# When the engines' registers are loaded in two mixture-of-experts parts: one value per tile behind four first ones, in place of thirteen at a time

## The chip, the cores and the metric

The kernel runs on one core of one Trainium2 chip. Its time is the device time of one execution in microseconds (us). "Time before" is the median of three runs. The profile is of one further execution.

## The reference, cut to what matters

The program is one long chain of eight residual parts on 2048 tokens of 128 values: a state-space (Mamba) part, a top-2 mixture of eight experts, a linear attention, a gated top-2 mixture of eight experts, and four more parts. Only the two mixtures hold the change. For each token they choose two of eight experts, and add the weighted sum of those experts' answers:

```python
def body(acc, p):                      # first mixture: relu, with biases
    w1e, b1e, w2e, b2e, ce = p
    h = jax.nn.relu(xf @ w1e + b1e)    # 128 -> 512
    y = h @ w2e + b2e                  # 512 -> 128
    return (acc + y * ce[:, None], None)
...
def body(acc, inputs):                 # second mixture: gated, no biases
    wg, wu, wd, w = inputs
    h = jax.nn.silu(xf @ wg) * (xf @ wu)
    acc = acc + w[:, None] * (h @ wd)
    return (acc, None)
```

The weight `ce` or `w` of a token is zero for all but its two experts, so a kernel may compute only those two.

## The kernel before, in words

Each mixture has a routing and an expert part. The routing finds the two experts of every token and its place in a list sorted by expert. GpSimd (POOL) then sends each token's row to its two places in a DRAM tensor, `slots`, with 32 indirect DMAs (`scatter`). The list is cut into tiles of 128 rows, so that each tile belongs to one expert. There are at most NT = 2 * 16 + 8 - 1 = 39 tiles, and the program always runs 39.

Which expert a tile belongs to is known only at run time. VectorE (DVE) computes two tables of 39 integers each in SBUF: `whoi`, the expert of each tile, and `basei`, the tile's first row in `slots`. `s_table` counts 2 when both are there. An engine that wants to use such an integer in an address must first have it in one of its own registers. `values(...)` does this: it emits one register load (TENSOR_LOAD, all of them at line L1407) for a stretch of a table on one engine. Three engines need it: SyncE (SP) for the row in `slots` that its DMA reads, DVE for the expert whose weights it copies and whose biases it adds, and TensorE (PE) for the expert whose `wd` it reads. On PE the load stands in the stream of the engine's sequencer, which the trace calls PEldq.

The function `experts` runs the two expert parts, the first with `gated` false, the second with `gated` true. For tile i the steps are:

- SP: `dma_start(xg[i] <- slots)`, L1431, 12 buffers (NB). From tile 12 on it waits until the answer of tile i - 12 has gone out.
- PE `turn_x` (L1521): transposes the rows. ScalarE (ACT) takes them out of PSUM (L1470).
- DVE `copy_weights` (L1612 and L1613): copies the expert's weights to a fixed place, `wac` (and `wuc` in the gated part), 2 buffers. It goes by the register with the expert of tile i.
- PE `hidden` (L1528, and L1534 in the gated part): the first product. It waits for the transposed rows and for `wac` (`s_wc`).
- DVE `inner` (L1626 or L1621) with ACT relu (L1480) or silu (L1475): the activation.
- PE `down` (L1543): the second product, whose weights are addressed by the register with the tile's expert.
- DVE `weigh` (L1639 or L1634), in the first part ACT `share_of` (L1487) too; POOL sends the answers out (L1457).

The engines run a software pipeline, written out in program order per engine. In step i PE does `turn_x(i + 2)`, `hidden(i + 1)`, `down(i - 1)`, and DVE does `copy_weights(i + 2)`, `inner(i + 1)`, `weigh(i - 1)`. Each engine's sequencer takes its instructions in order: what stands behind a register load is not given to the engine before the load is done. What was given before it goes on.

Before the change each engine loads its 39 values in three groups of 13. DVE loads right ahead of `copy_weights` of tiles 0, 13 and 26, PE ahead of `down` of tiles 13 and 26 (and once at the start), SP ahead of the DMA of tiles 0, 13 and 26. In the second part DVE also has memsets for the next part behind `weigh`, from `early.zeros` (`next(zeros, None)`).

Of the kernel before, what the change touches and what calls it, by code (L numbers as in the profile page):

```python
# [30 lines left out]
ENGINE = mybir.EngineType  # L31
EVERY_ENGINE = [ENGINE.PE, ENGINE.Activation, ENGINE.Pool, ENGINE.DVE, ENGINE.SP]

P = 128
# [8 lines left out]
class Core:  # L43
# [76 lines left out]
    def sb(self, name, shape, dt=F32, ctx=None):  # L120
        return (ctx or self.ctx).enter_context(self.nc.sbuf_tensor(name, shape, dt))

    def sem(self, name):
        handle = self.nc.alloc_semaphore(name=name)
        self.part_sems.append(handle)
        return handle
# [1207 lines left out]
def experts(k, r, early, first):  # L1334


    nc, t, C, T, E = k.nc, k.t, k.C, k.T, k.E
# [2 lines left out]
    FB = F // P  # L1340
    ROW = k.ROW
    NT = 2 * T + E - 1
    NB, NY, NH, GROUP = 12, 6, 3, 13
    slots, answers = k.slots[name], k.answers[name]
    tmp = ExitStack()
    sb = lambda n, shape, dt=F32: k.sb(f"{name}_{n}", shape, dt, tmp)
# [2 lines left out]
    def wait(engine, sem, count):  # L1349

        if count > 0:
            engine.wait_ge(sem, count)

    with tmp:
# [12 lines left out]
        whoi, basei = sb("whoi", [P, NT], U32), sb("basei", [P, NT], U32)  # L1367
        xg = sb("xg", [P, NB, ROW])
# [19 lines left out]
        s_ld = [sem(f"load{b}") for b in range(NB)]  # L1388
# [8 lines left out]
        def loaded(engine, i):  # L1397
            engine.wait_ge(s_ld[i % NB], 16 * (i // NB + 1))

        def sent_out(engine, i):  # L1400
            if i >= 0:
                engine.wait_ge(s_out[i % NY], 16 * (i // NY + 1))

        def values(engine, table, i, top_value):

            reason = "counted up to the number of tiles, and the expert is held below their number"
            return nc.values_load_multi_w_load_instructions(  # L1407
                table[0:1, i:min(i + GROUP, NT)], engines=[engine], min_val=0, max_val=top_value,
                skip_runtime_bounds_check_because=reason)[1]

        def fetch_answers(engine, j):
            rows_of_all = answers[j * k.N:(j + 1) * k.N, :].rearrange("(p t) d -> p t d", t=T)
            for c in range(C):
                engine.dma_start(back[:, c, j], rows_of_all[:, of(c), :]).then_inc(s_back[c], 16)

        with nc.Block() as block:
            @block.sync
            def _(sp):
                for dst, src in weights:
                    sp.dma_start(dst, src).then_inc(s_w, 16)  # L1420
                if early:
                    early.load(sp)

                sp.wait_ge(s_table, 2)
                for i in range(NT):
                    if i % GROUP == 0:
                        rows_of = values(ENGINE.SP, basei, i, slots.shape[0] - P)
                    if i == 0:
                        sp.wait_ge(r.s_sent, 16 * 2 * T)
                    sent_out(sp, i - NB)  # L1430
                    sp.dma_start(xg[:, i % NB, :], slots[bass.ds(rows_of[i % GROUP], P), :]).then_inc(s_ld[i % NB], 16)  # L1431
                for i in range(NT - NY, NT):
                    sent_out(sp, i)
                fetch_answers(sp, 0)
                for c in range(C):
                    sp.wait_ge(s_back[c], 16 * 2)
# [69 lines left out]
            @block.tensor  # L1506
            def _(pe):
                for c in range(first, C):
                    r.ranks(pe, c)
                    if c + 1 < C:  # L1510
                        r.turn(pe, c + 1)
                        r.gate(pe, c + 1)
                pe.wait_ge(r.s_pick, C + 1)
                nc.tensor.matmul(bank[5][:, 0:E], k.onesb[:], r.before[:, C, :], start=True, stop=True).then_inc(r.s_rank, 1)

                experts_of = {}

                def turn_x(i):
                    loaded(pe, i)
                    wait(pe, s_xT, i)  # L1520
                    nc.tensor.transpose(bank[0][:, 0:P], xg[:, i % NB, 0:P], k.ident[:]).then_inc(s_tx, 1)  # L1521

                def hidden(i):
                    pe.wait_ge(s_xT, i + 1)
                    pe.wait_ge(s_wc, i + 1)
                    wait(pe, s_h1, i - 1)
                    for f in range(FB):
                        last = nc.tensor.matmul(bank[1 + i % 2][:, f * P:(f + 1) * P], wac[:, i % 2, f * P:(f + 1) * P],  # L1528
                                                xgT[:, i % 2, :], start=True, stop=True)
                    last.then_inc(s_g, 1)  # L1530
                    if gated:
                        wait(pe, s_hT, i - 1)
                        for f in range(FB):
                            last = nc.tensor.matmul(bank[3 + i % 2][:, f * P:(f + 1) * P], wuc[:, i % 2, f * P:(f + 1) * P],  # L1534
                                                    xgT[:, i % 2, :], start=True, stop=True)
                        last.then_inc(s_u, 1)

                def down(i):
                    pe.wait_ge(s_hT, i + 1)
                    wait(pe, y_read, i - 1)  # L1540
                    one = bass.ds(experts_of[i], 1)
                    for f in range(FB):
                        last = nc.tensor.matmul(bank[6 + i % 2][:, 0:P], hT[:, i % NH, f, :],  # L1543
                                                wd[:, one, f, :].rearrange("p o d -> p (o d)"),
                                                start=(f == 0), stop=(f == FB - 1))
                    last.then_inc(s_y, 1)

                pe.wait_ge(s_w, 16 * len(weights))
                pe.wait_ge(s_table, 2)
                experts_of.update(enumerate(values(ENGINE.PE, whoi, 0, E - 1)))  # L1550
                for i in range(-2, NT + 1):
                    if 0 <= i + 2 < NT:
                        turn_x(i + 2)
                    if 0 <= i + 1 < NT:
                        hidden(i + 1)
                    if 0 <= i - 1:
                        if i > 1 and (i - 1) % GROUP == 0:
                            experts_of.update(enumerate(values(ENGINE.PE, whoi, i - 1, E - 1), i - 1))
                        down(i - 1)

            @block.vector
            def _(dve):
# [42 lines left out]
                experts_of = {}  # L1605

                def copy_weights(i):
                    one = bass.ds(experts_of[i], 1)
                    flat = lambda w: w[:, one, :].rearrange("p o f -> p (o f)")
                    wait(dve, hidden_done, i - 1)  # L1610
                    if gated:
                        v.tensor_copy(wuc[:, i % 2, :], flat(wu))  # L1612
                    v.tensor_copy(wac[:, i % 2, :], flat(wa)).then_inc(s_wc, 1)  # L1613
# [15 lines left out]
                def weigh(i):  # L1629
                    dve.wait_ge(s_y, i + 1)  # L1630
                    if gated:
                        loaded(dve, i)
                        sent_out(dve, i - NY)
                        v.tensor_scalar(yw[:, i % NY, :], bank[6 + i % 2][:, 0:P], xg[:, i % NB, P + 1:P + 2], None, ALU.mult)\  # L1634
                            .then_inc(s_yw, 1)
                    else:
                        wait(dve, s_yw, i - 1)
                        bias = bd[:, bass.ds(experts_of[i], 1), :].rearrange("p o d -> p (o d)")
                        v.tensor_tensor(yb[:, i % 2, :], bank[6 + i % 2][:, 0:P], bias, ALU.add).then_inc(s_yb, 1)  # L1639

                dve.wait_ge(s_w, 16 * len(weights))
                dve.wait_ge(s_table, 2)
                zeros = early.zeros(v) if early else iter(())
                for i in range(-2, NT + 1):
                    if 0 <= i + 2 < NT:
                        if (i + 2) % GROUP == 0:
                            experts_of.update(enumerate(values(ENGINE.DVE, whoi, i + 2, E - 1), i + 2))
                        copy_weights(i + 2)
                    if 0 <= i + 1 < NT:
                        inner(i + 1)  # L1650
                    if 0 <= i - 1:
                        weigh(i - 1)
                    if i >= 0:
                        next(zeros, None)

# [1585 lines left out]
def program(nc, t, out):  # L3241
    with ExitStack() as ctx:
        k = Core(nc, ctx, t)
        routing = Routing(k, "moe0", gated=False)
        mamba(k, routing)
        k.part_sems += routing.sems
        experts(k, routing, None, first=1)
        k.end_part()

# [133 lines left out]
```

## Time and profile before

| | |
|---|---|
| time, median of 3 runs | 1362.14 us (1360.49 to 1362.29) |
| span of the profiled execution | 1358.3 us, 3.8 us under that median |
| the profiled execution's own time outside its span | not given; the span is all that the page has of it |
| PE busy | 79% of the span |
| DVE busy | 65% |
| ACT busy | 50% |
| POOL busy | 41% |
| first expert part, PE from the first to the last transposed tile | 372.4 to 453.7 us |
| gated expert part, the same | 570.8 to 681.9 us |

"Busy" counts the instructions of the engines. Register loads and other sequencer work are not counted, so such a load shows as idle time of the engine behind it, with "issue" as the releaser or with the last semaphore that was waited for before. The letter q behind an engine's name marks its sequencer. "PEld" is the weight load of TensorE, which runs ahead of its matmul.

### The profile page before, as it was taken

The numbers are of one execution on the slowest core, as the hardware profiler recorded it, in microseconds if no ns is written. First come the engines' busy times: TensorE is split into PE (matmuls) and PEld (weight loads), VectorE is DVE, ScalarE is ACT, GpSimd is POOL, SyncE is SP. The second block draws the span as 40 slices with busy tenths as digits, with TensorE's granted clock in tenths as the row PEclk, the third lists the DMA queues.
The fourth block names the chain that finished last, engine by engine and source line by source line (L and its number), as shares of the span: only waits on it lengthen the run. The fifth ranks groups of instructions, "written<-read, shape, count | busy, mean of one in ns | idle before, by whom it ended". The sixth has DMA issues, their size and how long they took to land. (4 is left out here: it accounts for less than half of the span.)

```text
span 1358.3 us, 25046 instructions
## 1 busy us (share of the span) xinstructions
PE 1079.5 (79%) x8292; PEld 708.4 (52%) x8292; DVE 881.0 (65%) x2989; ACT 685.8 (50%) x1268; POOL 559.6 (41%) x740
## 2 busy tenths in 40 slices
PE   8877777778189553299936999969977999899998
PEld 3222232336188553299934777744434777654544
DVE  6799999976455456377549888843648878840201
ACT  4786656644044301133206888737856888541221
POOL 4489988853633314544426444100025555100000
PEclk9799999998599765599978999989997999999999
DMA  2997000002422206211120000020612000000000
GB/s 63 206 202 126 0 1 0 1 0 71 140 61 57 92 7 219 70 41 44 37 74 1 2 3 3 2 53 6 203 47 89 3 2 3 2 1 0 16 0 16
DMA packets 85742, 66.77 MB, mean 49 GB/s; under 512 B 15102, under 2 KB 70412, under 8 KB 85612
## 3 DMA queue, kind: packets, MB, share of 16 engines
q1 hardware_dynamic: 79916, 53.65, 17.3%
q0 software_dynamic: 4544, 9.38, 1.9%
q10 hardware_dynamic: 1152, 2.10, 0.4%
q8 instruction: 70, 1.15, 0.4%
q14 instruction: 60, 0.49, 0.1%
HBM read 36.52 MB, written 28.59 MB: 48 GB/s over the span
## 5 line engine op out<-in xcount | busy, mean ns | idle before, releaser
L1076 POOL TENSOR_TENSOR hC<-h,Cs 128x1024 f32<-128x1024 f32 x64 | 150.8, 2356 | 35.3 <-DVE h L973 34.7
L786 PE MATMUL bank<-hC,ident 128*128 128x512 f32 x256 | 128.1, 624 | 45.1 <-POOL hC L1076 43.0
L973 DVE TENSOR_TENSOR_SCAN h<-bank,state,dBx 128x512 f32<-128x512 f32 x128 | 157.3, 1271 | 2.2
L1457 POOL DMA_INDIRECT moe_answers<-moe_yw,moe_xg x78 | 83.7, 1073 | 128.9 <-DVE moe_yw L1634 70.9
L2608 DVE CUSTOM_DVE_ANT_0 decay_below<-bank,decay_q_mask 128x256 bf16<-128x256 f32 x256 | 97.3, 419 | 23.3 <-PE bank L2420 22.4
L786 PEld LDWEIGHTS bank<-hC,ident 128*128 128x128 f32 x256 | 44.9, 192 | 103.9 <-POOL hC L1076 67.1
L2608 DVE CUSTOM_DVE_ANT_0 window_below<-bank,window_q_mask 128x192 bf16<-128x192 f32 x256 | 80.3, 353 | 28.6 <-PE bank L2420 27.0
L2548 ACT ACTIVATE decay_pb<-bank 128x512 f32<-128x512 f32 x128 | 76.2, 598 | 33.5 <-PE bank L2435 32.6
L885 ACT ACTIVATE bank<-dt,A 128x512 f32<-128x512 f32 x128 | 83.2, 683 | 18.7 <-DVE h L973 17.4
L1528 PE MATMUL bank<-moe_xgT,moe_wac 128*128 128x128 f32 x624 | 86.4, 284 | 6.5 <-issue 4.0
L1543 PE MATMUL bank<-moe_wd,moe_hT 128*128 x624 | 83.2, 278 | 5.7 <-DVE moe_hT L1621 2.5
L1528 PEld LDWEIGHTS bank<-moe_xgT,moe_wac 128*128 128x128 f32 x624 | 79.5, 200 | 7.4 <-issue 4.5
L1543 PEld LDWEIGHTS bank<-moe_wd,moe_hT 128*128 128x128 f32 x624 | 76.5, 193 | 6.5 <-issue 6.5
L2548 ACT ACTIVATE window_pb<-bank 128x384 f32<-128x384 f32 x128 | 62.3, 491 | 34.4 <-PE bank L2435 32.4
L3235 DVE TENSOR_TENSOR f_ys<-bank,f_s 128x256 f32<-128x256 f32 x8 | 3.4, 425 | 117.3 <-PE bank L3178 117.3
L1330 POOL DMA_INDIRECT moe_slots<-moe_rows,moe_slot x64 | 62.3, 973 | 31.1 <-issue 16.6
L241 POOL TENSOR_TENSOR rstd<-veps,mhalf 128x4 f32<-128x4 f32 (+1 forms) x12 | 14.8, 1237 | 138.9 <-DVE veps L235 138.9
L1470 ACT ACTIVATE moe_xgT<-bank 128x128 f32<-128x128 f32 x78 | 20.9, 268 | 97.7 <-PE bank L1521 97.5
L963 DVE TENSOR_TENSOR dBx<-dtx,bank 128x768 f32<-128x768 f32 (+1 forms) x64 | 65.2, 1019 | 1.2 <-PE bank L766 0.7
L910 ACT ACTIVATE Cs<-bank 128x512 f32<-128x512 f32 x64 | 38.1, 596 | 39.0 <-POOL hC L1076 31.4
L1521 PE MATMUL bank<-ident,moe_xg 128*128 128x128 f32 x78 | 22.5, 288 | 43.0 <-DMA moe_xg<-moe_slots 41.7
L3169 PE MATMUL bank<-f_hA,f_h1w 128*128 128x512 f32 x128 | 55.3, 592 | 0.0
(482 smaller groups left out, 2797.2 us busy)
## 6 DMA issues: line engine op xcount, KB each, us to landing
moe_slots<-blank SPq DMA_DIRECT2D x16, 1040.0 KB, 16.9
deep_rows<-token_weights SPq DMA_DIRECT2D x32, 256.0 KB, 3.9
moe_xg<-moe_slots SPq DMA_DIRECT2D x78, 65.0 KB, 1.9
moe_wa<-in_moe_w SPq DMA_DIRECT2D x2, 2048.0 KB, 9.7
moe_back<-moe_answers SPq DMA_DIRECT2D x8, 256.0 KB, 5.3
moe_back<-moe_answers ACTq DMA_DIRECT2D x8, 256.0 KB, 6.0
moe_wu<-in_moe_wu SPq DMA_DIRECT2D x1, 2048.0 KB, 15.4
deep_w<-in_deep_w SPq DMA_DIRECT2D x3, 512.0 KB, 6.5
```

The source lines that it names most:

```text
L786: last = nc.tensor.matmul(sum_bank(hh)[:], k.ident[:], hC[:, u % 2, hh, :], start=(n == 0), stop=(n == NS - 1))
L885: nc.scalar.activation(decay_bank(u, hh)[:], dt[:, hh, cols(c)], ACT.Exp, scale=A[:, hh, n:n + 1]).then_inc(q_dA, 1)
L963: v.tensor_tensor(dBx[:, u % 2, :, 0:w], dtx[:, :, c * CW:c * CW + w], b_bank[:, None, 0:w].to_broadcast([P, H, w]), ALU.mult).then_inc(q_ ...
L973: v.tensor_tensor_scan(h[:, u % 2, hh, :], decay_bank(u, hh)[:], dBx[:, u % 2, hh, :], state[:, n, hh:hh + 1], ALU.mult, ALU.add).then_inc ...
L1076: g.tensor_tensor(hC[:, u % 2], h[:, u % 2], Cs[:, u % 2, None, :].to_broadcast([P, H, CW]), ALU.mult).then_inc(q_hC, 1)
L1330: k.nc.gpsimd.indirect_dma_start(k.slots[self.name], index, self.rows[j][:, i, :], None)\
L1457: nc.gpsimd.indirect_dma_start(answers, bass.IndirectOffsetOnAxis(index, 0), yw[:, i % NY, :], None)\
L1528: last = nc.tensor.matmul(bank[1 + i % 2][:, f * P:(f + 1) * P], wac[:, i % 2, f * P:(f + 1) * P], xgT[:, i % 2, :], start=True, stop=True)
L1543: last = nc.tensor.matmul(bank[6 + i % 2][:, 0:P], hT[:, i % NH, f, :], wd[:, one, f, :].rearrange("p o d -> p (o d)"), start=(f == 0), st ...
L2548: nc.scalar.activation(pb[:, w % 4, :], bank[2 + w % 2][:, 0:2 * HW], ACT.Exp).then_inc(s_ex, 1)
L2608: last = nc.vector.tensor_tensor_reduce(out=below[:, 2 * g + j, :], in0=bank[g % 2][:, j * HW:(j + 1) * HW], in1=q_mask[:], scale=-1.0, sc ...
L3169: last = k.nc.tensor.matmul(bank[4 + m % 4][:], self.hw[layer][:, i, f * P:(f + 1) * P], src[:, i, :], start=(i == 0), stop=(i == FB - 1))
```

## The change

The number GROUP = 13 goes, and LEAD = 4 comes. Each of the three engines first loads the values of tiles 0 to 3 in one load. The values of tiles 4 to 38 are then loaded one at a time. SP loads the one of tile i ahead of that tile's DMA (and ahead of its wait for tile i - 12). PE and DVE load the one of tile i + 3 at the end of step i, behind `down(i - 1)` and `weigh(i - 1)`. For DVE this is right ahead of `copy_weights` of the same tile in step i + 1; for PE it is three steps and more ahead of `down` of that tile.

```diff
-    NB, NY, NH, GROUP = 12, 6, 3, 13
+    NB, NY, NH, LEAD = 12, 6, 3, 4
...
-        def values(engine, table, i, top_value):
+        def values(engine, table, i, m, top_value):
...
-                table[0:1, i:min(i + GROUP, NT)], engines=[engine], min_val=0, max_val=top_value,
+                table[0:1, i:i + m], engines=[engine], min_val=0, max_val=top_value,
...
+                rows_of = dict(enumerate(values(ENGINE.SP, basei, 0, LEAD, slots.shape[0] - P)))
                 for i in range(NT):
-                    if i % GROUP == 0:
-                        rows_of = values(ENGINE.SP, basei, i, slots.shape[0] - P)
+                    if i >= LEAD:
+                        rows_of[i] = values(ENGINE.SP, basei, i, 1, slots.shape[0] - P)[0]
...
-                experts_of.update(enumerate(values(ENGINE.PE, whoi, 0, E - 1)))
+                experts_of.update(enumerate(values(ENGINE.PE, whoi, 0, LEAD, E - 1)))
...
                     if 0 <= i - 1:
-                        if i > 1 and (i - 1) % GROUP == 0:
-                            experts_of.update(enumerate(values(ENGINE.PE, whoi, i - 1, E - 1), i - 1))
                         down(i - 1)
+                    if LEAD <= i + 3 < NT:
+                        experts_of[i + 3] = values(ENGINE.PE, whoi, i + 3, 1, E - 1)[0]
...
+                experts_of.update(enumerate(values(ENGINE.DVE, whoi, 0, LEAD, E - 1)))
...
                     if 0 <= i + 2 < NT:
-                        if (i + 2) % GROUP == 0:
-                            experts_of.update(enumerate(values(ENGINE.DVE, whoi, i + 2, E - 1), i + 2))
                         copy_weights(i + 2)
...
                     if 0 <= i - 1:
                         weigh(i - 1)
+                    if LEAD <= i + 3 < NT:
+                        experts_of[i + 3] = values(ENGINE.DVE, whoi, i + 3, 1, E - 1)[0]
                     if i >= 0:
                         next(zeros, None)
```

## Rows read from the trace of the kernel before

**Rows 1.** The head of the page.

```profile
span 1358.3 us, 25046 instructions
```

**Rows 2.** Waits of PE, 379 to 455 us: total us, times, longest.

```profile
PE bank L1528 <- issue: 4.0, 2, 2.1
PE bank L1543 <- ACT moe_hT L1480: 1.9, 1, 1.9
PE bank L1543 <- issue: 1.3, 1, 1.3
```

**Rows 3.** The same view, 578 to 683 us.

```profile
PE bank L1543 <- DVE moe_hT L1621: 2.5, 2, 1.3
PE bank L1528 <- ACT moe_xgT L1470: 2.5, 2, 1.3
```

**Rows 4.** L1521 on PE in four stretches: min/median/max ns, first to last start.

```profile
L1521 PE MATMUL bank<-ident,moe_xg x35: 272/273/421, 379.3 to 453.7; 128*128 128x128 f32 x35
...
L1521 PE MATMUL bank<-ident,moe_xg x10: 272/273/273, 408.4 to 425.5; 128*128 128x128 f32 x10
...
L1521 PE MATMUL bank<-ident,moe_xg x36: 272/273/273, 578.3 to 681.9; 128*128 128x128 f32 x36
...
L1521 PE MATMUL bank<-ident,moe_xg x9: 272/273/273, 620.4 to 642.7; 128*128 128x128 f32 x9
```

**Rows 5.** Register loads of L1407: three engines, whole span; two single ones.

```profile
L1407 SPq TENSOR_LOAD <-moe_basei x6: 1304/2757/2770, 358.9 to 624.4; - x6
L1407 DVEq TENSOR_LOAD <-moe_whoi x6: 1144/3010/3209, 359.0 to 645.7; - x6
L1407 PEldq TENSOR_LOAD <-moe_whoi x6: 1257/3127/3194, 359.0 to 655.2; - x6
...
L1407 DVEq TENSOR_LOAD <-moe_whoi x1: 3141/3141/3141, 396.7 to 396.7; - x1
...
L1407 PEldq TENSOR_LOAD <-moe_whoi x1: 3194/3194/3194, 403.9 to 403.9; - x1
```

**Rows 6.** Register loads of one value, L2814, a later part of the kernel.

```profile
L2814 SPq TENSOR_LOAD <-blank x1: 277/277/277, 908.8 to 908.8; - x1
...
L2814 DVEq TENSOR_LOAD <-blank x1: 308/308/308, 908.8 to 908.8; - x1
L2814 PEldq TENSOR_LOAD <-blank x1: 306/306/306, 908.9 to 908.9; - x1
```

**Rows 7.** Timeline at a load of DVE: start, duration, [idle before].

```profile
400.01 0.43 DVE L1613 COPY moe_wac<-moe_wa 128x512 f32 x1 [3.03 <-issue]
...
400.50 0.97 PEld L1528 LDWEIGHTS bank<-moe_xgT,moe_wac 128*128 128x128 f32 x8 [2.20 <-issue]
```

**Rows 8.** Busy time in a stretch; behind POOL, the granted clock.

```profile
430.50:434.00 3.50, 3.50 (x19) 3.50 (x19) 1.62 (x4) 2.00 (x6) 1.92 (x2) 0.53 0.16 45
```

**Rows 9.** Timeline of an undisturbed tile, first part: DVE, then PEld.

```profile
412.50 0.29 DVE L1639 TENSOR_TENSOR moe_yb<-bank,moe_bd 128x128 f32<-128x128 f32 x1 [0.20 <-PE bank L1543]
412.70 0.42 DVE L1613 COPY moe_wac<-moe_wa 128x512 f32 x1
...
414.08 0.41 PEld L1528 LDWEIGHTS bank<-moe_xgT,moe_wac 128*128 128x128 f32 x3
```

**Rows 10.** Timeline of an undisturbed tile, gated part: DVE, then PEld.

```profile
614.62 0.41 DVE L1613 COPY moe_wac<-moe_wa 128x512 f32 x1
...
616.12 0.30 PEld L1528 LDWEIGHTS bank<-moe_xgT,moe_wac 128*128 128x128 f32 x2
```

**Rows 11.** PE's sequencer, same tile as rows 9: `down`'s last address work, next waits.

```profile
L1543 PEldq FUSED_REGOPS  x1: 46/46/46, 412.4 to 412.4; - x1
...
L1352 PEldq EVENT_SEMAPHORE  x2: 51/51/51, 413.4 to 413.6; - x2
```

**Rows 12.** SP's DMA issues of L1431: first twelve tiles, the other 27.

```profile
L1431 SPq DMA_DIRECT2D moe_xg<-moe_slots x12: 333/333/353, 370.5 to 376.7; - x12
...
L1431 SPq DMA_DIRECT2D moe_xg<-moe_slots x27: 332/333/333, 384.9 to 444.1; - x27
```

More of the change, by code:

```diff
@@ L1430, in _ @@
                     sent_out(sp, i - NB)
-                    sp.dma_start(xg[:, i % NB, :], slots[bass.ds(rows_of[i % GROUP], P), :]).then_inc(s_ld[i % NB], 16)
+                    sp.dma_start(xg[:, i % NB, :], slots[bass.ds(rows_of[i], P), :]).then_inc(s_ld[i % NB], 16)
                 for i in range(NT - NY, NT):
```

## The prediction

> **What bounds the kernel now.** The page gives a span of 1358.3 us [rows 1]; the median of the runs shown is 1362.14 us, 3.8 us more. The change touches only the two expert parts, so I read those. The first view is the waits of PE, once for each part. In the first part, from the fifth tile on, PE is idle four times for 4.0 + 1.9 + 1.3 = 7.2 us [rows 2]; in the gated part four times for 5.0 us [rows 3]. There are no other waits of PE in either stretch. So outside these eight places PE sets the pace, and whatever is taken from it comes off the end: nothing of the next part starts before the last tile is through.
>
> The second view says what a stall costs, its after-effects included: the starts of PE's transposes, of which each tile has one. Undisturbed, nine intervals take 425.5 - 408.4 = 17.1 us, 1.90 us a tile; in the gated part eight take 22.3 us, 2.79 us a tile [rows 4]. The first part has 34 intervals from 379.3 to 453.7 us, 74.4 us; at 1.90 they would take 64.6 us, so 9.8 us are lost. The gated part has 35 from 578.3 to 681.9 us, 103.6 us; at 2.79 they would take 97.6 us, so 6.0 us are lost. The sum is 15.8 us.
>
> The third view says who causes it: the register loads. In each part every engine has three, so four of each engine's six stand in mid-loop; the median shows that these take about 3.0 us on DVE and 3.1 us on PE, whereas those before the loops take from 1.1 us on [rows 5]. One of DVE's runs from 396.7 for 3.14 us, to 399.85; the copy of the weights behind it starts at 400.01, and PE's weight load that needs the copy at 400.50 [rows 5, 7]. The page puts "issue" there because no semaphore was late, only the sequencer. One of PE's runs from 403.9 to 407.1 us, and `down` stands behind it [rows 5]; that is the 1.9 us put down to ACT [rows 2], whose value had long been there. Two engines with two such loads in each of two parts make eight, which is the count of PE's waits.
>
> PE's idle time is 12.2 us and the loss 15.8 us. A part of the difference is the clock: from 430.5 to 434.0 us, just after the second stall by DVE (PE had been idle for about 2 us), the granted clock was 0.53 [rows 8], near the lower level of 1.2 GHz, with PE busy all the time. That disappears with its stall.
>
> **Removed.** Two mid-loop loads of 13 values on each engine and part. On PE and DVE they cost the 15.8 us above. On SP they take 2.76 us, but SP's last transfer is issued at 444.1 us for a tile that PE turns at 453.7 [rows 4, 12], a lead of 9.6 us: nothing is won there. The gain is 15.8 us if what is added is covered.
>
> **Added.** 35 loads of one value on each of three engines in each part. The price of one: the only ones of one value in the trace took 0.277 (SP), 0.308 (DVE) and 0.306 us (PE), with idle engines [rows 6]. Thirteen in mid-loop took 2.76 us on SP, so twelve more values cost 2.48 us, 0.21 us each. On a working DVE thirteen took 3.14 us, 1.14 times SP's price. I take 0.308 x 1.14 = 0.35 us for DVE and PE. The bounds are 0.28 us below, and above 1.14 us, the shortest load in the expert parts [rows 5], of 13 values. The single loads are far nearer in kind, hence 0.35. In the sum of its loads DVE gets more sequencer time, about 35 x 0.35 = 12 us a part for some 7.5 (two of 3.1 and the first one) [rows 5]; what counts is where it lies.
>
> *DVE, first part.* The load stands behind `weigh`, which is given out at 412.50, and pushes back the copy behind it, which ends at 413.12 [rows 9]. PE's weight load wants that copy at 414.08. In the stall the copy ended at 400.44 and the weight load began at 400.50 [rows 7], so it needs 0.06 to 0.07 us. Cover: 414.08 - 0.07 - 413.12 = 0.89 us. With 0.35 us the copy ends at 413.47, while PE's sequencer comes to its own waits at 413.4 to 413.6 anyway [rows 11]. The load costs nothing and 0.54 us of cover is left. Behind the load in the queue are the copy, the next bias addition and the next `weigh`. A load longer than 0.89 us costs PE its excess at every tile.
>
> *DVE, gated part.* The same reckoning: copy done at 615.03, wanted at 616.12 less 0.07 [rows 10]. Cover 1.02 us, nothing lost. The memsets behind the load write tiles of a later part.
>
> *PE.* The sequencer has done the last address work of `down` at 412.4 us and next does something at 413.4, the waits for the turned rows and the copy [rows 11]. The load falls into this stretch of about 0.9 us, in which it waits anyway. Beyond that, the engine has work in its queue until the weight load at 414.08 that starts the next `hidden` [rows 9]. Cover about 1.5 us. The value is needed by `down` three steps later. Cost nothing.
>
> *SP.* Twelve transfers went out in 6.2 us [rows 12]. Eight of them now have a load ahead: 8 x 0.28 = 2.2 us more, so the twelfth leaves at 378.9 in place of 376.7 us, for the twelfth tile, which is turned at 379.3 + 7 x 1.90 = 392.6 us [rows 4]. From tile 12 on, the load stands ahead of the wait for a free buffer, and falls into that wait. Cost nothing.
>
> *The first load*, of four in place of 13 values, ends sooner. SP issues its first transfer only at 370.5 us, when the table has been read for ten microseconds [rows 5, 12], since the rows must have been scattered. Gain nothing.
>
> The Trainium skill speaks against the change: "DMA: Bandwidth & Descriptors", section Latency and other measured facts, puts a floor of some 600 ns under a tensor_load and says that loads are grouped to amortize it. The rows of one value lie at half of that [rows 6]. By the page, as an estimate, the added loads would take 0.6 us, DVE's cover in the first part would shrink to 0.29 us, and the time would be the same as long as nothing else lies in it.
>
> **The sum.** 1358.3 - 15.8 + 0 = 1342.5 us of span, and 1362.1 - 15.8 = 1346.3 us of time.
>
> **The rivals.**
>
> *The loads on a busy engine are dearer, and part of the gain leaks.* For: on DVE and PE thirteen values took 0.25 to 0.45 us longer than on SP, and the rows of one value are from idle engines; if that surplus is a fixed price per load, one takes 0.6 to 0.75 us. Against: even that is under 0.89. At the upper bound, 1.14 us, each tile of the first part loses 0.25 us and each gated one 0.12: 35 x 0.37 = 13.0 us, and the time is 1359.3 us. Chance 0.12 for 1351.5 to 1359.3 us, and 0.05 for the little beyond that ends within 0.2% of the time before.
>
> *The other side: a load in mid-loop has its price per load, not per value.* Then a single one on DVE takes 3.14 us in the first part and 3.01 in the gated one, and holds back the copies of every tile: 35 x (3.14 - 0.89) + 35 x (3.01 - 1.02) = 78.8 + 69.7 = 148.5 us, less 15.8, so 1495 us. It decides from 35 x (d - 0.89) + 35 x (d - 1.02) = 15.8 on, which is d = 1.18 us; from 1.22 us on the kernel is slower by over 0.2%. For: 13 values took 1.1 to 1.4 us in one place and 3.0 to 3.2 in another, so something beside their number matters. Against: SP, which has nothing else to do, shows the same factor of two with hardly any scatter, so that it is not the load on the engine, and one value took 0.3. Chance 0.05.
>
> *The clock's fall is not the stall's.* Then 3.5 x (1 - 0.53) = 1.6 us remain [rows 8], and it is 1347.9 us. Against: it followed upon an idle PE. It lies within the range of the likeliest case.
>
> **How the numbers follow.** The likeliest case, full cover, has 0.78: 1346.3 us, from 1344 (the three runs before differ by 1.8 us) to 1351.5 us (about 0.07 us lost at each of 70 tiles). The leaks have 0.17, the dear load 0.05. The range of eight in ten is the likeliest one's. Within 0.2%, 2.7 us, a measurement of this kernel can't tell a change from none. Faster 0.78 + 0.12 = 0.90, same 0.05, slower 0.05.
>
> **What would show it.** Right: transposes 1.90 and 2.79 us apart throughout; no wait of PE over some tenths in either stretch; loads of one value of 0.3 to 0.4 us, the first part's copy of the weights later by that, its end still ahead of PE; no stretch at half clock after 378 us. The step on the price is wrong if DVE's single loads take over 0.9 us; the step on the cover is wrong if the copy waits longer than the load or the tile interval grows by even 0.1 us. The prediction fails if SP's lead at the end is gone, or if the transposes still have gaps at tiles 13 and 26.

## The result, and the profile after

The changed kernel takes 1347.95 us (median of four runs, 1346.86 to 1349.12), the kernel before took 1361.9 us beside it (1360.49 to 1362.29). The ratio is 0.9898, with a 95% interval of 0.9881 to 0.9916: faster by 1.0%, or 13.95 us. The forecast was 1346.3 us, in a range of 1344.0 to 1351.5. In the changed kernel the lines behind the loop of SP are one higher: L1521 is L1522, L1613 is L1614, and so on.

The head of the page, and PE's waits from the fifth tile on in the first part (380 to 446 us) and in the gated part (567 to 667 us). The second view has its header and no row; it was the same for both stretches.

```profile
span 1345.2 us, 25235 instructions
```

```profile
core 0 of [0], span 1345.2 us
engine line waited for: us in total, times, longest us
```

Before, these stretches had eight waits and 12.2 us [rows 2, 3]. None is left. The transposes, again with the first and the last start of each stretch:

```profile
L1522 PE MATMUL bank<-ident,moe_xg x35: 272/273/273, 379.6 to 444.1; 128*128 128x128 f32 x35
...
L1522 PE MATMUL bank<-ident,moe_xg x36: 272/273/273, 567.4 to 665.0; 128*128 128x128 f32 x36
```

The 34 intervals take 64.5 us where they took 74.4, and the 35 gated ones 97.6 where they took 103.6 [rows 4]. So 9.9 + 6.0 = 15.9 us came from just where the sum put 15.8. The register loads of L1407:

```profile
L1407 SPq TENSOR_LOAD <-moe_basei x72: 268/277/497, 358.2 to 644.6; - x72
L1407 DVEq TENSOR_LOAD <-moe_whoi x72: 300/304/646, 358.2 to 665.2; - x72
L1407 PEldq TENSOR_LOAD <-moe_whoi x72: 295/302/567, 358.3 to 663.0; - x72
```

There are twelve times as many as before [rows 5]; the medians are 0.28 us on SP and 0.30 us on DVE and PE, as the idle engines' loads of one value took [rows 6]. The timeline of one tile of the first part shows how the load on DVE is covered (DVE's rows, then PEld's):

```profile
402.67 0.29 DVE L1640 TENSOR_TENSOR moe_yb<-bank,moe_bd 128x128 f32<-128x128 f32 x1 [0.20 <-PE bank L1544]
403.17 0.43 DVE L1614 COPY moe_wac<-moe_wa 128x512 f32 x1 [0.20 <-issue]
...
404.26 0.41 PEld L1529 LDWEIGHTS bank<-moe_xgT,moe_wac 128*128 128x128 f32 x3
```

The copy starts 0.50 us after the start of `weigh`, in place of 0.20 [rows 9]: later by the 0.30 us of the load. Only 0.20 us of it show as idle time ("issue"); the rest runs beside `weigh`. The copy ends at 403.60, and PE takes it up at 404.26, so 0.59 us of cover is left after the 0.07 us of hand-over, where the forecast said 0.54. SP's issues:

```profile
L1432 SPq DMA_DIRECT2D moe_xg<-moe_slots x12: 333/333/353, 369.9 to 378.5; - x12
...
L1432 SPq DMA_DIRECT2D moe_xg<-moe_slots x39: 332/333/353, 369.9 to 434.8; - x39
```

Twelve take 8.6 us in place of 6.2 [rows 12], 2.4 us more for 2.2 forecast, and the last leaves 9.3 us ahead of the last transpose: SP's loads cost nothing either.

**Where 2.8 us of the span are.** The span fell by 1358.3 - 1345.2 = 13.1 us, not by 15.9. From the last transpose of the gated part to the end it was 1358.3 - 681.9 = 676.4 us before and 1345.2 - 665.0 = 680.2 us after, 3.8 us more, in parts that the change does not touch; the stretches outside these three are together 1.0 us shorter. One piece of them is longer too, at the start of the first part: the interval behind the fourth transpose (376.7 to 379.6 us) took 2.9 us, where it was 2.0 us before (377.3 to 379.3 us). In the windows of the two intervals, the changed kernel's first, the last three columns are granted clock, DMA share and GB/s:

```profile
376.70:379.60 2.90, 2.90 (x18) 2.82 (x18) 1.59 (x3) 0.80 (x2) 0.00 (x0) 0.67 0.36 79
```

```profile
377.33:379.32 1.99, 1.99 (x18) 1.99 (x19) 1.28 (x3) 0.79 (x2) 0.00 (x0) 1.00 0.28 68
```

In the changed kernel the clock was still at its lower level of 1.2 GHz for most of it, after the engine had idled for 21 us ahead of the part; before, it was at its higher level throughout. Whether this and the 3.8 us belong to the change was open, and e10_before_again and e11_after_again were made for it.

### The profile page after: what moved, and what is told of

Same layout as the page of the kernel before. It is cut to its first block and busy times, and to the rows that moved or that the text cites. A ratio compares the mean times of both kernels' runs of the same rounds, so it can differ in the third digit from the quotient of the medians.

```text
span 1345.2 us, 25235 instructions
## 1 busy us (share of the span) xinstructions
PE 1074.5 (80%) x8283; PEld 706.9 (53%) x8292; DVE 882.3 (66%) x2989; ACT 685.6 (51%) x1268; POOL 559.1 (42%) x740
## 3 DMA queue, kind: packets, MB, share of 16 engines
q8 instruction: 70, 1.15, 0.4%
## 5 line engine op out<-in xcount | busy, mean ns | idle before, releaser
L786 PEld LDWEIGHTS bank<-hC,ident 128*128 128x128 f32 x256 | 45.2, 192 | 103.6 <-POOL hC L1076 66.2
L1522 PE MATMUL bank<-ident,moe_xg 128*128 128x128 f32 x78 | 22.5, 288 | 42.7 <-DMA moe_xg<-moe_slots 41.8
```

What stands on the lines that cost most here:

```text
L786: last = nc.tensor.matmul(sum_bank(hh)[:], k.ident[:], hC[:, u % 2, hh, :], start=(n == 0), stop=(n == NS - 1))
```

## The experiments

All times are medians; the ratios are to the kernel before, run on the same chip. "w8" and the like are names of mine for a load's width.

**One engine at a time.** Two kernels put the new loads on one engine and leave the groups of thirteen on the other two. For TensorE (and in the same way, at its place, for VectorE):

```diff
-                experts_of.update(enumerate(values(ENGINE.PE, whoi, 0, E - 1)))
+                experts_of.update(enumerate(values(ENGINE.PE, whoi, 0, E - 1, LEAD)))
...
-                        if i > 1 and (i - 1) % GROUP == 0:
-                            experts_of.update(enumerate(values(ENGINE.PE, whoi, i - 1, E - 1), i - 1))
                         down(i - 1)
+                    if LEAD <= i + 3 < NT:
+                        experts_of[i + 3] = values(ENGINE.PE, whoi, i + 3, E - 1, 1)[0]
```

> Only TensorE loads one value per tile; VectorE and SyncE keep their groups of thirteen. Theory (the eight stalls are the mid-loop loads of TensorE and VectorE, each with its own share): TensorE's four loads cost some 6.7 us of the 15.8, so about 1355 us, with the gaps left at tiles 13 and 26 where VectorE loads. Rival (the stalls are one joint wait, which needs both engines mended): nothing won, 1361 us or more.

Measured: 1355.72 us (1354.14 to 1358.32, 8 runs), ratio 0.9945 (0.9929 to 0.9961). That is 7.9 us under the kernel before on that chip (1363.65 us), where 6.7 were expected. PE's waits in the first part, 385 to 455 us, and in the gated part, 570 to 680 us, and the transposes of both:

```profile
PE bank L1528 <- issue: 4.1, 2, 2.0
...
PE bank L1528 <- issue: 1.3, 1, 1.3
PE bank L1528 <- ACT moe_xgT L1470: 1.2, 1, 1.2
...
L1521 PE MATMUL bank<-ident,moe_xg x35: 272/273/273, 382.2 to 451.2; 128*128 128x128 f32 x35
...
L1521 PE MATMUL bank<-ident,moe_xg x36: 272/273/273, 574.1 to 674.6; 128*128 128x128 f32 x36
```

Only the four waits ahead of `hidden` (L1528) are left, which is where DVE's copies are wanted; those ahead of `down` are gone.

> Only VectorE loads one value per tile. Theory: its four loads and the fall of the clock behind the second of them cost some 9.1 us, so about 1353 us, and no stretch at half clock in the middle of the first expert part. Rival (the fall of the clock has nothing to do with the stall): it stays, and the time is 1.6 us higher.

Measured: 1356.42 us (1352.91 to 1357.48, 10 runs), ratio 0.995 (0.9934 to 0.9966), some 3 us more than expected: 7.2 us under the kernel before on that chip, where 9.1 were expected. The waits of both parts, 382 to 450 and 573 to 680 us, and the transposes:

```profile
PE bank L1543 <- ACT moe_hT L1480: 3.9, 2, 2.0
...
PE bank L1543 <- DVE moe_hT L1621: 2.6, 2, 1.3
...
L1521 PE MATMUL bank<-ident,moe_xg x35: 272/273/273, 377.7 to 446.6; 128*128 128x128 f32 x35
...
L1521 PE MATMUL bank<-ident,moe_xg x36: 272/273/273, 571.3 to 672.0; 128*128 128x128 f32 x36
```

The mirror image: the four waits ahead of `down` (L1543) stay. The names behind the arrow are those of semaphores long given; the releaser is PE's own load. So each engine's load makes its own stalls, and the two shares add up. Against the undisturbed 64.5 and 97.6 us, e1_pe_only loses 4.5 + 2.9 = 7.4 us to DVE's four loads, and e2_dve_only 4.4 + 3.1 = 7.5 us to PE's. In neither did the clock fall in these stretches. The shares are alike, then, and not 9.1 and 6.7 us as expected; the two profiled spans (1354.3 and 1351.4 us) differ by what lies outside these stretches. The 15.9 us of the kernel before are these 14.9 us and 1.0 us for its one fall of the clock.

**How much a load on DVE may take.** The changed kernel, with each of DVE's later loads widened to four neighbouring values (eight in e4_dve_w8), of which the last is used:

```diff
-                        experts_of[i + 3] = values(ENGINE.DVE, whoi, i + 3, 1, E - 1)[0]
+                        start = max(0, i + 4 - 4)
+                        experts_of[i + 3] = values(ENGINE.DVE, whoi, start, i + 4 - start, E - 1)[-1]
```

> The changed kernel, but each of VectorE's loads behind the first takes four neighbouring values (the last one is used). Theory (0.21 us per value more, cover 0.89 us in the first part and 1.02 us in the gated part): one load takes 0.30 + 3 x 0.21 = 0.93 us, just over the first cover, so 1 to 2 us slower than the changed kernel, about 1349 us. Rival (cover much smaller than worked out, say 0.4 us, since the sequencer has other work in it): 35 x 0.5 us and more are lost, 1366 us or more. Rival on the price (only loads whose start is not aligned pay per value): every fourth load is short.

Measured: 1350.8 us (1346.45 to 1351.52), ratio 0.9911 (0.9881 to 0.9942). Three neighbouring loads, the transposes of the first part and PE's waits there:

```profile
L1407 DVEq TENSOR_LOAD <-moe_whoi x1: 960/960/960, 382.3 to 382.3; - x1
...
L1407 DVEq TENSOR_LOAD <-moe_whoi x1: 349/349/349, 384.2 to 384.2; - x1
...
L1407 DVEq TENSOR_LOAD <-moe_whoi x1: 962/962/962, 386.2 to 386.2; - x1
...
L1522 PE MATMUL bank<-ident,moe_xg x31: 272/273/273, 385.8 to 445.0; 128*128 128x128 f32 x31
...
PE bank L1529 <- issue: 0.7, 2, 0.4
```

Two things are seen. The interval is 59.2 / 30 = 1.97 us, 0.08 over the undisturbed one. Half of that is two intervals of 2.54 and 2.45 us, whose cause is open; the others are mostly 1.94 to 2.04 us, or 1.90 as without loads. So 0.96 us is just over the cover, as worked out from 0.89 us. And every fourth load, whose start is a multiple of four values, takes 0.35 us in place of 0.96, the last rival's mark.

> The same with eight values per load. Theory: 0.30 + 7 x 0.21 = 1.77 us a load, over the cover by 0.88 us in the first part (35 times, 30.8 us) and by 0.75 us in the gated part (26 us): tile intervals of 2.78 and 3.54 us, about 1405 us in all, the price that the prediction's other side was about. Rival (in the gated part the load overlaps VectorE's own work, so that the cover is about 1.3 us): gated interval 3.25 us and about 1395 us.

Measured: 1374.49 us (1373.57 to 1374.87), ratio 1.0084 (1.0053 to 1.0115): slower than the kernel before, but less than either theory said. The long loads take 1.84 to 1.98 us in the first part and 1.84 us in the gated one, and every fourth, aligned load 0.61 us. Two single loads, those from 395 to 437 us, and the transposes in the middle of the two parts:

```profile
L1407 DVEq TENSOR_LOAD <-moe_whoi x1: 609/609/609, 385.4 to 385.4; - x1
...
L1407 DVEq TENSOR_LOAD <-moe_whoi x1: 1972/1972/1972, 387.4 to 387.4; - x1
...
L1407 DVEq TENSOR_LOAD <-moe_whoi x18: 598/1849/1971, 395.0 to 436.9; - x18
...
L1522 PE MATMUL bank<-ident,moe_xg x17: 272/273/273, 391.9 to 431.1; 128*128 128x128 f32 x17
...
L1522 PE MATMUL bank<-ident,moe_xg x16: 272/272/273, 612.2 to 658.8; 128*128 128x128 f32 x16
```

The intervals are 39.2 / 16 = 2.45 and 46.6 / 15 = 3.11 us. Set against 1.90 and 2.79 us, and with three long loads in four tiles, a long load costs (2.45 - 1.90) x 4 / 3 = 0.73 us and (3.11 - 2.79) x 4 / 3 = 0.43 us. So, of a long load, on average about 1.2 us were covered in the first part and 1.4 us in the gated one. In the first part it is the load behind a short one that costs 1.0 us, what the forecast cover of 0.89 us gives for it (intervals of 2.9 us); the next two cost 0.55 and 0.66 us each (2.45 and 2.57 us). The rival was right on the gated part: there DVE still worked on `inner` and `weigh` from 615.45 to 616.39 us beside a load that began at 615.2. The expected total was too high for this and for the aligned loads.

**The same on PE**, eight values:

> The changed kernel, but each of TensorE's loads behind the first takes eight neighbouring values, some 1.77 us. Theory (cover of 1.5 us in the first part, work queued in the engine included, and about 2 us in the gated part): over it by 0.3 us in the first part alone, 35 x 0.3 = 10 us, about 1358 us. Rival (only the sequencer's idle stretch of 0.9 us covers): 35 x 0.9 = 30 us in the first part and as much in the gated part, 1390 us and more.

Measured: 1377.57 us (1375.8 to 1378.93), ratio 1.0098 (1.0072 to 1.0123). Three of its loads, and the transposes:

```profile
L1407 PEldq TENSOR_LOAD <-moe_whoi x3: 597/2022/2053, 385.5 to 390.3; - x3
...
L1522 PE MATMUL bank<-ident,moe_xg x16: 272/300/301, 392.5 to 431.3; 128*128 128x128 f32 x16
...
L1522 PE MATMUL bank<-ident,moe_xg x16: 273/300/302, 610.6 to 655.4; 128*128 128x128 f32 x16
```

The total lies between the 1358 us of the theory and the 1390 us and more of the rival. The intervals are 38.8 / 15 = 2.59 and 44.8 / 15 = 2.99 us. A long load costs 0.92 us in the first part and 0.27 us in the gated one, so PE's cover is 2.0 - 0.9 = 1.1 us and 1.7 us. In the first part it is nearer to the sequencer's idle stretch of 0.9 us than to the 1.5 us of the forecast; in the gated part nearer to the theory. The work queued in the engine covers less than I had counted.

**Why thirteen values took 1.1 to 1.4 us once and 3 us elsewhere.** Three kernels are the one before with one number changed, to 12, 16 and 32:

```diff
-    NB, NY, NH, GROUP = 12, 6, 3, 13
+    NB, NY, NH, GROUP = 12, 6, 3, 12
```

> The kernel before with groups of twelve in place of thirteen: loads start at tiles 0, 12, 24 and 36, that is at bytes 0, 48, 96 and 144 of the table. Open is why thirteen values took 1.1 to 1.4 us ahead of the loops and 2.8 to 3.2 us in mid-loop. Theory L (the start has to be aligned to 16 bytes for several values per read): all loads are short, about 1.2 us, and nearly all stalls go: about 1350 us. Theory M (a load that crosses a border of 64 bytes pays per value): the loads at 12 and 24 take some 2.6 us. Theory N (a load in mid-loop is dear since the SBUF is busy): the same 2.6 us, and the load of three at 36 takes 0.7 us. M and N: about 1359 us.

> The kernel before with groups of sixteen: loads start at bytes 0, 64 and 128. Theories L and M (alignment): loads of sixteen take 1.4 to 1.6 us in mid-loop too, the last of seven about 0.8 us, and the time is about 1350 us. Theory N (mid-loop): 3.4 us for sixteen and 1.5 for seven, and about 1360 us.

> The kernel before with one load of 32 values ahead of the loop, where it is covered by the scatter of the rows, and one of seven in mid-loop. If the first load costs 0.1 us per value it ends at 362 us, if 0.21 at 366 us, both ahead of the first transfer at 370 us: nothing lost there. Alignment theories: the load of seven takes 0.8 us, less than the cover, and the time is that of the changed kernel, 1348 us. Mid-loop theory: 1.5 us twice per part, 2 us more: 1350 us.

DVE's loads in the three kernels (12: all eight; 16: all six; 32: all four), min/median/max:

```profile
L1407 DVEq TENSOR_LOAD <-moe_whoi x8: 756/848/1120, 368.0 to 661.7; - x8
```

```profile
L1407 DVEq TENSOR_LOAD <-moe_whoi x6: 1047/1134/1369, 360.4 to 649.5; - x6
```

```profile
L1407 DVEq TENSOR_LOAD <-moe_whoi x4: 1041/1628/2418, 364.3 to 650.0; - x4
```

| groups of | loads of one stretch | time, us | ratio (95% interval) |
|---|---|---|---|
| 12 | 12 values 0.84 to 1.12 us, 3 values 0.76 and 0.85 | 1347.25 | 0.9872 (0.9848 to 0.9897) |
| 16 | 16 values 1.10 to 1.37 us, 7 values 1.05 and 1.16 | 1347.02 | 0.9885 (0.9858 to 0.9911) |
| 32 | 32 values 2.10 to 2.42 us ahead of the loop, 7 values 1.04 and 1.15 | 1349.35 | 0.9895 (0.9872 to 0.9918) |

Theory L holds: what counts is whether the start lies at a multiple of four values, that is of 16 bytes, counted from the start of the table. (Where the tables lie in SBUF was not looked at.) Theory M falls, since the loads of twelve at bytes 48 and 96 cross borders of 64 bytes and are short. Theory N falls, since all these loads but the first stand in mid-loop. From an aligned start each full four costs about 0.25 us (0.35 for four, 0.61 for eight, 0.85 for twelve, 1.10 for sixteen); the values left over cost 0.21 us each, as all of them do from an unaligned start (0.30 for one, 0.96 for four, 1.84 for eight, 3.0 for thirteen). Thirteen puts the second group at byte 52 and the third at byte 104, neither of them aligned. Twelve and sixteen values in mid-loop take about as long as the cover, so nearly all of the eight stalls go with them too.

**A version with both.** Four values at an aligned start, every fourth tile, on all three engines (VectorE's edit is like TensorE's):

```diff
-                    if i >= LEAD:
-                        rows_of[i] = values(ENGINE.SP, basei, i, 1, slots.shape[0] - P)[0]
+                    if i >= LEAD and i % 4 == 0:
+                        rows_of.update(enumerate(values(ENGINE.SP, basei, i, 4, slots.shape[0] - P), i))
...
-                    if LEAD <= i + 3 < NT:
-                        experts_of[i + 3] = values(ENGINE.PE, whoi, i + 3, 1, E - 1)[0]
+                    if LEAD <= i + 3 < NT and (i + 3) % 4 == 0:
+                        experts_of.update(enumerate(values(ENGINE.PE, whoi, i + 3, 4, E - 1), i + 3))
```

> The changed kernel, but the loads behind the first take four values whose start is aligned to 16 bytes, at every fourth tile, on all three engines (0.35 us each, as the aligned ones of e3_dve_w4). Theory (the expert parts are bound by TensorE's own work once no load is longer than the cover): the same as the changed kernel within 0.2%, about 1348 us, tile intervals of 1.90 and 2.79 us. Rival (the sequencer time of 35 loads per engine and part is itself a cost): 1 us or more faster in the two expert parts.

Measured: 1347.91 us (1345.23 to 1349.05), ratio 0.9897 (0.988 to 0.9913). The loads and the first part's transposes:

```profile
L1407 DVEq TENSOR_LOAD <-moe_whoi x20: 340/342/842, 360.3 to 659.1; - x20
...
L1522 PE MATMUL bank<-ident,moe_xg x35: 272/273/273, 380.7 to 445.1; 128*128 128x128 f32 x35
```

The 34 intervals take 64.4 us, against 64.5 with 35 single loads. With nothing over the cover, the number of loads makes no difference. None of the experiments is measurably faster than the changed kernel.

**Both kernels once more.**

> The kernel before, profiled a second time, for two open points. First, what follows the last tile of the gated part took 676.3 us in its first profile and 680.2 us in that of the changed kernel. Theory (the clock's level where the later parts begin differs from execution to execution): here 678 to 680 us. Rival (the change lengthens the later parts): 676 us again. Second, the fall of the clock behind VectorE's second stall. If it belongs to the stall, the tile interval there is 4.9 us again; if it comes by chance, 4.1 us, and the stalls cost 14 to 15 us in all.

> The changed kernel once more, beside the other two: if what follows the gated part varies from execution to execution, it takes 678 to 680 us; if the change lengthens it, 680 us again. The time stays at 1347 to 1350 us.

Measured: the kernel before 1364.42 us in its single run, seven others on that chip 1360.9 to 1364.88 (median 1362.73); the changed kernel 1346.52 us, ratio 0.9884 (0.9859 to 0.9908). One of its four runs took 3468.57 us and is not explained; the other three are 1344.12, 1344.7 and 1348.34. Each profile's span and transposes of the gated part; for the kernel before also those of the first part, and two stretches at DVE's two loads there:

```profile
span 1362.7 us, 25037 instructions
```

```profile
L1521 PE MATMUL bank<-ident,moe_xg x36: 272/273/273, 578.7 to 682.4; 128*128 128x128 f32 x36
...
L1521 PE MATMUL bank<-ident,moe_xg x35: 272/273/421, 380.9 to 456.5; 128*128 128x128 f32 x35
...
399.90:405.50 5.60, 3.59 (x20) 3.38 (x18) 2.25 (x5) 1.72 (x5) 1.32 (x2) 0.72 0.15 43
...
430.10:435.30 5.20, 3.20 (x19) 2.99 (x18) 2.25 (x5) 1.70 (x5) 1.37 (x2) 0.79 0.16 41
```

```profile
span 1342.4 us, 25235 instructions
```

```profile
L1522 PE MATMUL bank<-ident,moe_xg x35: 272/273/273, 569.2 to 664.1; 128*128 128x128 f32 x35
```

Behind the last transpose the kernel before now took 1362.7 - 682.4 = 680.3 us, and the changed one 1342.4 - 664.1 = 678.3 us. So the 3.8 us that the first pair of profiles shows there are variation between executions, of either sign, and not the change's. In the thirteen profiles of all kernels this piece takes 676.4 us once, in the first profile of the kernel before, and 678.3 to 680.3 us in the other twelve. The start of the first part varies too: the interval behind the fourth transpose is 1.99 us in both profiles of the kernel before and in this one of the changed kernel, but 2.57 to 2.88 us in six of the thirteen, with both kinds of loads among them.

The clock fell behind both of DVE's stalls in the first part here; in the first profile it did behind one of two, and in e1_pe_only behind neither (its stalled intervals were both 4.2 us). It never fell behind the stalls ahead of `down`, the two of 2.0 us in e2_dve_only included, nor behind DVE's shorter ones in the gated part, nor in mid-part in a kernel without stalls. With two falls the stalls of this execution cost 75.6 - 64.5 = 11.1 and 103.7 - 97.6 = 6.1 us, 17.2 in all. So without a fall it is 14.9, with one 15.9, with two 17.2 us: a fall costs 1.0 to 1.2 us.

## Why the prediction was right

- **What bounds it.** PE's own work, but for eight places: shown. With the loads mended the intervals are 1.90 and 2.79 us throughout and no wait is left. e1 and e2 show that the stalls are those of two engines, four each, and independent.
- **What the stalls cost.** 15.8 us worked out, 15.9 us between the first pair of profiles. The time fell by 13.95 us, 1.9 us less, and between the second pair the span fell by 20.3 us. The sum was made against one execution, which happened to have one fall of the clock and so the middle one of 14.9, 15.9 and 17.2 us. What else the times differ by lies outside the two stretches, where executions of one kernel differ by 2 us and more. That the forecast came within 1.7 us of the time is in part luck.
- **The fall of the clock.** I gave it wholly to the stall and to each execution alike. In mid-part it was seen only behind a stall, but it followed in three of six of DVE's stalls in the first part. The rival put its price at 1.6 us; it is 1.0 to 1.2 us. The stall by DVE and the interval behind it did grow by 1.7 us (4.95 + 2.77 us where the first stall had 4.12 + 1.90), but PE's own stall behind it was shorter by 0.65 us (interval 3.45 for 4.10 us). The sign "no stretch at half clock after 378 us" did not hold to the letter: the changed kernel's clock rose only at 378.6 us in its first profile. That is the start of the part, and no fall.
- **The price of a single load.** 0.35 us taken, 0.30 measured. The 14% between a working DVE and SP was counted twice. It is the difference between the two engines, idle or not, and was in the 0.308 us already: one value took 0.308 and 0.277 us idle, 0.304 and 0.277 working.
- **The cover.** On DVE in the first part 0.89 us worked out; the load of 0.96 us is just over it, and of loads of 1.9 us 1.2 were covered on average. In the gated part 1.02 was too low, it is 1.4. On PE 1.5 was too high, it is 1.1 in the first part. All are well over 0.30, so the time does not tell. The step on PE was too generous, and only the short load made it harmless.
- **The other side.** The thing "beside their number" that I left open is the alignment of the start, not the place in the loop. A price per load was ruled out: one value took 0.30 us at any start. Its mechanism exists all the same: with loads of 1.8 to 2.1 us (e4, e8) the kernel is slower than before by 0.8 and 1.0%.
- **The floor.** The 600 ns that the Trainium skill gives for a tensor_load ("DMA: Bandwidth & Descriptors", Latency and other measured facts) does not hold for these loads from SBUF: the 72 on each engine, 70 of them of one value, have medians of 277 to 304 ns. The Trainium skill's page "Runtime: NRT & Kernel Launch", section Instruction fetch mechanics, says about 200 ns per register for a load even in bulk; that page speaks of the runtime's own loads from HBM. The loads from SBUF come near it with 0.21 us per further value from an unaligned start; from an aligned one sixteen values took 1.10 us, 0.07 us each.
- **SP and the first load.** Nothing, as forecast.

## What to carry to other kernels

A register load blocks its engine's sequencer, so it is free only while the sequencer would wait anyway or the engine still has work in its queue; look in the timeline for how long that is, and keep each load shorter. Start loads of several values at a multiple of 16 bytes from the table's start: here, GROUP = 12 or 16 in place of 13 wins as much as the whole change. When stalls of a few microseconds are removed, the clock's falls behind them go too, but in some executions only, so compare several profiles before you explain a difference of 2 us.

## What the runs showed of the hardware

- A TENSOR_LOAD of table values from SBUF takes about 0.25 us for each full four values when its start is a multiple of 16 bytes from the table's start: from 0.35, 0.61, 0.85 and 1.10 us on for 4, 8, 12 and 16 values on DVE, against 0.96, 1.84 and 3.0 us on for 4, 8 and 13 from other starts. It looks as if four were read at once; that was not shown.
- It does not drain the engine: in the four stalls by PE's loads in the kernel before, PE worked on for 1.5 to 2.2 us after its load began, and then stood idle until the load of 3.1 to 3.2 us was done.
- After an idle stretch of PE of about 2 us ahead of `hidden` in the first part the granted clock fell to 1.2 GHz three times in six; after stretches of 1.2 to 2.0 us ahead of `down` (twelve of them) it never did. What decides it was not found.
